# A cross-attention loop reordered: two units of row scores ahead of a key unit, two transposes moved beside others

## What is computed

```python
ci = rms_norm(hidden_states, ln_post_cross_w)
cq = heads(ci @ cq_w, NH, CHD)                      # 16 heads of 16
ck, cv = split(encoder_outputs @ ckv_w, 2)          # 375 keys and values
scores = einsum('bhqd,bhkd->bhqk', q * scale, k)
p = softmax(scores, axis=-1)
cctx = einsum('bhqk,bhkd->bhqd', p, v)
hidden_states = hidden_states + cctx @ cdense_w
```

## Time and profile before

| what | us |
|---|---|
| three runs | 2242.75, 2247.61, 2244.96 |
| median of the runs | 2244.96 |
| span of the profiled execution | 2242.0 |
| PE busy in the span | 2122.6 (95%) |
| DVE busy | 1323.9 (59%) |
| ACT busy | 1056.6 (47%) |
| POOL busy | 887.2 (40%) |

### The profile page before, as it was taken

One profiled execution on the slowest core, in us unless ns is written; L12 is line 12 of the kernel. 1 busy time (PEld: TensorE's weight loads), 2 busy tenths in 40 slices (PEclk: granted clock), 3 DMA queues, 4 the chain that ended last, 5 costly groups with the idle time before them and its releaser, 6 DMA issues.

```text
span 2242.0 us, 40571 instructions
## 1 busy us (share of the span) xinstructions
PE 2122.6 (95%) x16042; PEld 1821.8 (81%) x16042; DVE 1323.9 (59%) x1910; ACT 1056.6 (47%) x1875; POOL 887.2 (40%) x741
## 2 busy tenths in 40 slices
PE   7999998999978989997999999988999999999998
PEld 6899997777757777996888888877888888888887
DVE  6665547878769995545666666663434344444343
ACT  5344434333258775542665555544434333343333
POOL 2211116776624433543111111104555554555556
PEclk9999999999989999998999999999999999999999
DMA  6443434655464445656777777745343443434333
GB/s 237 134 144 116 138 128 148 232 196 207 175 207 137 141 143 226 249 198 193 229 222 225 215 209 215 212 131 188 114 130 116 128 160 113 139 118 129 113 95 118
DMA packets 155613, 373.70 MB, mean 167 GB/s; under 512 B 40160, under 2 KB 60992, under 8 KB 145696
## 3 DMA queue, kind: packets, MB, share of 16 engines
q1 hardware_dynamic: 136416, 310.70, 44.0%
q0 software_dynamic: 18720, 60.29, 7.4%
q10 hardware_dynamic: 288, 0.11, 0.0%
HBM read 269.28 MB, written 100.93 MB: 165 GB/s over the span
## 4 chain that ended last, share of the span: by engine, by line
PE 76%; DVE 17%; DMA 3%; ACT 1%; issue 1%; SPq 1%; POOL 0%; POOLq 0%; DVEq 0%; ACTq 0%
PE ps L111 19%; PE ps L113 19%; PE ps L112 19%; PE ps L1847 5%; DVE f_arena L1080 4%; PE ps L1879 3%; PE ps L1866 3%; DVE f_arena L1310 2%; DVE c_max L1305 2%; PE ps L688 2%; DVE e_negmax L1969 2%; DVE f_arena L1076 1%; DMA f_arena<-qk_rows 1%; DVE f_arena L1072 1%; DVE c_sum L1316 1%
## 5 line engine op out<-in xcount | busy, mean ns | idle before, releaser
L111 PE MATMUL ps<-r_arena 128*128 128x512 f32 (+6 forms) x2410 | 897.3, 372 | 28.1 <-DVE r_arena L179 11.5
L112 PE MATMUL ps<-r_arena 128*128 128x512 f32 (+6 forms) x2410 | 884.0, 367 | 0.0
L113 PE MATMUL ps<-r_arena 128*128 128x512 f32 (+6 forms) x2410 | 883.8, 367 | 0.0
L179 POOL TENSOR_TENSOR r_arena<-f_arena,r_arena 128x512 fp32r<-128x512 f32 (+1 forms) x434 | 581.2, 1362 | 579.3 <-ACT r_arena L201 434.4
L111 PEld LDWEIGHTS ps<-r_arena 128*128 128x128 f32 (+2 forms) x2410 | 456.5, 189 | 99.7 <-DVE f_arena L1080 14.8
L113 PEld LDWEIGHTS ps<-r_arena 128*128 128x128 f32 (+2 forms) x2410 | 455.8, 189 | 66.3
L112 PEld LDWEIGHTS ps<-r_arena 128*128 128x128 f32 (+2 forms) x2410 | 456.9, 190 | 60.0
L201 ACT CAST r_arena<-f_arena 128x512 fp32r<-128x512 f32 x400 | 236.6, 622 | 192.9 <-PE ps L113 150.7
L1969 DVE TENSOR_REDUCE e_negmax<-ps 112x3 f32<-112x1125 f32 (+1 forms) x192 | 230.1, 1198 | 133.4 <-PE ps L1847 133.2
L2276 DVE SCALAR_TENSOR_TENSOR f_arena<-f_arena,ps 128x512 f32<-128x512 f32 (+1 forms) x88 | 57.5, 653 | 233.1 <-ACT f_arena L2171 228.2
L1762 ACT ACTIVATE f_arena<-ps 125x896 f32<-125x896 f32 x192 | 165.2, 915 | 44.0 <-PE ps L1866 44.0
(11 more groups left out here) (213 smaller groups left out, 2557.4 us busy)
## 6 DMA issues: line engine op xcount, KB each, us to landing
f_arena<-weights SPq DMA_DIRECT2D x400, 256.0 KB, 3.0
r_arena<-k_rows SPq DMA_DIRECT2D x192, 188.0 KB, 3.6
k_rows<-r_arena SPq DMA_DIRECT2D x64, 376.0 KB
f_arena<-rows SPq DMA_DIRECT2D x14, 1160.0 KB, 5.2
f_arena<-qk_rows SPq DMA_DIRECT2D x32, 448.0 KB, 4.1
f_arena<-mem_n SPq DMA_DIRECT2D x8, 1536.0 KB, 6.9
f_arena<-mem_e SPq DMA_DIRECT2D x32, 376.0 KB, 4.7
f_arena<-mem_t SPq DMA_DIRECT2D x16, 750.0 KB, 5.7
```

Of the source, the lines that this page charges most:

```text
L111: first = pe.matmul(out, w_hi, x_hi, start=start, stop=False)
L112: pe.matmul(out, w_hi, x_lo, start=False, stop=False)
L113: return first, pe.matmul(out, w_lo, x_hi, start=False, stop=stop)
L179: return engine.tensor_tensor(out, source, high.bitcast(F32), ALU.subtract)
```

## The change

The order of five calls in PE's list and of two in DVE's is changed in each step; no instruction is added or removed. `scores(s, 1)` now stands ahead of `maximum_turn(s-1)`, and on DVE `maximum(s, 1)` ahead of `maximum_turned(s-1)`. `queries_turn(s+2)` stands ahead of `scores(s, 2)`. `scores(s, 4)` stands ahead of `scores_by_key(s-1, 2)`, and `scores(s, 5)` ahead of `dense(s-2, 1)`.

```diff
                 if old:
                     context(s - 2, 0)
                     context(s - 2, 1)
+                if now:
+                    scores(s, 1)
                 if by_key:
                     maximum_turn(s - 1)
-                if now:
-                    scores(s, 1)
                 if old:
                     turn(s - 2)
...
+                if new:
+                    queries_turn(s + 2)
                 if now:
                     scores(s, 2)
                 if new:
-                    queries_turn(s + 2)
                     values(s + 2, range(NKC))
...
                 if old:
                     dense(s - 2, 0)
-                if by_key:
-                    scores_by_key(s - 1, 2)
                 if now:
                     scores(s, 4)
                 if by_key:
+                    scores_by_key(s - 1, 2)
                     scores_by_key(s - 1, 3)
+                if now:
+                    scores(s, 5)
                 if old:
                     dense(s - 2, 1)
-                if now:
-                    scores(s, 5)
                 if by_key:
                     scores_by_key(s - 1, 4)
                     scores_by_key(s - 1, 5)
...
                 if s < BATCHES:
                     maximum(s, 0)
+                    maximum(s, 1)
                 if 1 <= s <= BATCHES:
                     maximum_turned(s - 1)
-                if s < BATCHES:
-                    maximum(s, 1)
```

## The result

The changed kernel takes 2261.65 us (median of 4 runs, 2258.49 to 2265.53) against 2245.64 us for the kernel before in the same comparison: 16 us slower, ratio 1.007, 95% interval 1.0057 to 1.0083. The forecast was 2257.5 us, +12.6. The profiled execution is the slowest of the four runs (2265.53); two of the others lie near 2258.5, and no trace tells what a step takes in those.

What follows compares the result with a forecast made beforehand. PE, 95% busy, bounds the kernel, with SP's placement DMAs close behind. 28 steps x 0.45 = 12.6 us on 2242.0 gives 2254.6; the median lies 2.96 above, so 2257.5 us, range 2243 to 2270.

Steps and rivals of the forecast that it cites:

- The delay: SP's issue of the maxima moves from S + 3.76 to S + 5.35, 1.6 us later; S is unit 0's start.
- The step: Unit 0 to maxima's issue 5.35, to last placement landing 10.41, release 0.04: 15.80 us mean against 15.35, 0.45 lost a step.
- The prediction's other cycle, 15.68: Same SP path with the skill's 2.13 us for every last landing: cycle 15.68, loss 0.33 a step, 9 us in all.
- The floor of 15.25: Shortest step allowed when the 20 landing paths were taken one by one, set by the reordered tail on PE: 15.25 us.
- Part 1 on PE at 0: Unit 1 of the row scores ahead of the turn of the maxima: PE gains 0 to 0.15 us, taken as 0.
- Part 2 at 0: Turn of the queries ahead of unit 2: DVE's maximum of unit 2 starts 0.2 us later; cost by itself 0.
- Part 3 at a gain of 0.1: Units 4 and 5 moved in the tail: handover idle 0.47 gone, new waits 0.3 and 0.2; gain 0.1 us a step.
- The last steps at 0: The last two steps, like the first ones, have the same work as before: 0 change.
- (a): Placements on SP stay hidden and the tail counts: 0.1 a step, 2242 us; chance 0.13 with other small sums.
- (b): Placements and both new tail waits hidden, the turn's 0.15 saved: 0.3 to 0.45 us a step faster, 2236.5 us; chance 0.10.
- (c): PE's granted clock falls to 0.9 on the mean: 1.5 us more a step, 2287 us; chance 0.02.
- (d): Tail waits larger than worked out and placements landing late too: 0.9 us a step, 2270 us; chance 0.04.

Runs made afterwards that it cites:

- part 1 alone: Kernel before, only with unit 1 ahead of the turn of the maxima on PE and its maximum ahead of the copy on DVE: 2266.77 us against 2245.40.
- DVE's order back: Changed kernel with the copy of the turned maxima again ahead of the maximum of unit 1 on DVE, PE's new order kept: 2244.65 us against 2245.40 before.
- the wait on SP alone: Kernel before, only SP also waits for the maximum of unit 1 ahead of the DMA of the maxima: 2261.66 us against 2246.09.
- the key DMAs put ahead: Changed kernel with the six key DMAs of the next sequence ahead of the DMA of the maxima on SP: 2245.42 us against 2246.09 before.
- part1_undone: Changed kernel with unit 1 and its maximum back in their old places, the other moves kept: 2244.43 us against 2245.40 before.
- the tail alone: Kernel before with only units 4 and 5 of the row scores moved as in the change: 2240.85 us against 2245.40, ratio 0.9974.

## Why the prediction was right, and where not

**Direction and cause** were right, and shown in four ways (part 1 alone, DVE's order back, the wait on SP alone, the key DMAs put ahead). What made the forecast possible was a path that the chain of before never touched, with 1.2 us of mean slack (1.1 by the landings read one by one, below) against a delay of 1.6.

**The delay.** S + 5.35 was worked out, S + 5.47 measured, in the step shown and on the mean of the 28: unit 1 takes 0.69 on the chain instead of 0.52, its first weight load exposed, which puts its end at S + 0.76 + 2.44 + 0.69 = S + 3.89 and the DMA a little beyond the upper bound of S + 5.42.

**The step.** 15.80 was worked out, 16.00 measured in the profiled execution, so 0.65 a step instead of 0.45 and 18.2 us instead of 12.6. Of the 0.20, 0.12 is the later start of the DMA. The other 0.08 is the path behind it, which the prediction took as 10.41 and which is 10.49 in the same 20 steps of the kernel before. It took the last landings as 2.1 to 3.0; two of the 20 took 3.2 and 3.3, which stood in answers on two issues at once as a median of 2.7. The last issue of the step of 1331.25, alone:

```profile
r_arena<-q_rows SPq DMA_DIRECT2D x1, 56.0 KB, 3.3
```

5.47 + 10.49 + 0.04 is 16.00. So the path itself did not change with the change: its issues take 8.81 us on the mean instead of 8.76. The prediction's other cycle, 15.68, comes to 15.62 by the same issues. The floor of 15.25 was too low as well (the seven steps that no DMA holds take 15.37 to 15.52), but it touches too few steps to count. The medians of the runs differ by 16.0 and not by 18.2; as the profile is of the slowest run, the 16.00 a step is at the upper end.

**Part 1 on PE at 0:** right. Unit 1 and the turn take 0.69 + 0.10 = 0.79 on the chain, before 0.25 + 0.52 = 0.77.

**Part 2 at 0:** this step failed. The prediction said that the earlier queries help nobody and that the later maximum of unit 2 "matters in part 3". It delays DVE's low part of keys and queries too, which is due at key unit 0: 0.13 a step alone, 0.16 with the new tail (15.38 - 15.22). With the new tail about half of it is seen at key units 0 and 1 (0.95 in a step of part1_undone, 0.87 in the tail alone); the wait of unit 4, where the prediction looked for it, hardly grew (0.62, 0.60).

**Part 3 at a gain of 0.1:** right, 0.12 alone. In the change part 2 takes it back, so parts 2 and 3 together give nothing (15.38 against 15.35), where the sum had 15.25.

**The last steps at 0:** in the profiled executions step 30 took 0.7 longer, by a lower granted clock (0.79 instead of 0.89). The prediction had no term for it.

**The rivals.** (a) did not come: the placements ended last in 21 of 28 steps. The waits behind (b) were not hidden. The clock of (c) was 1.00 in all 28 steps of the changed kernel, with 0.6 us of idle each; but the rival was not empty. With part 1 alone (0.8 us of idle a step) it fell to 0.90 in five steps and with the wait on SP alone in three, for 1.6 us each. (d) came in part: landings later than worked out, but no larger waits of the tail.

## What to carry to other kernels

A reordering on the busiest engine is priced by what its moved step releases on the slow queues: follow the semaphore to the DMA queue, count what is queued behind it, and compare the last landing with its reader, also where the chain of waits never shows that DMA. On an in-order queue put transfers whose data are ready ahead of a transfer that must wait; here that alone gave back the 16 us. When work is moved to cover a wait, let the cover reach past the end of the producer by a weight load: in this tail 0.92 us did not cover a maximum of 0.95, and 1.15 did. And read the landings of single DMAs, not the median of several, when the last one is what somebody waits for.

## What the runs showed of the hardware

A wait that leaves no idle time on PE can still cost. When the operand came 0.20 us ahead of PE's need instead of 0.39, the first weight load was exposed and two key units took 1.01 instead of 0.87 us.

DMA issues of one shape on SP take 0.51 to 0.59 us mostly, but up to 1.70 for queries and 2.12 for keys, with landings of the query DMAs of 2.1 to 3.8 us: a path made of 13 of them varies by over a microsecond from step to step, though the program repeats exactly. What makes a single issue long was not found.

A single wait of PE can be followed by a fall of the granted clock to 0.50, which costs more than the wait. With part 1 alone this came behind five waits of 1.18 to 1.42 us and made the next context 3.94 us instead of 2.44 in the step shown. But behind three others of 1.30, 1.41 and 1.51 us in the same trace the clock stayed at 1.00, and so it did behind 1.26 and 1.39 us in the changed kernel. The length of the wait does not decide it, and what does was not found.
